# Opening of a fused adaLN kernel re-ordered: x loaded in place, one-time steps moved, gates and weight rounding in 35 steps

## The reference, cut to what matters

```python
# x: (8, 1024, 128); DEPTH = 6 layers; HEADS = 8
mod = (silu(c) @ wmod).reshape(8, 6, 1, -1)      # sa, ca, ga, sb, cb, gb
ga = (2 * (ga >= 0) - 1) * maximum(abs(ga), 0.25)   # "gates"; the same for gb
h = layernorm(x) * (1 + ca) + sa                 # "front norm", once per batch
for i in range(6):                               # linear attention + MLP
    xn = layernorm(h, ln1_w[i], ln1_b[i])
    q, k, v = xn @ wq[i], xn @ wk[i], xn @ wv[i]
    h = linear_attn(softmax(q), softmax over rows(k), v) @ wo[i] + bo[i] + h
    hdn = leaky_relu(layernorm(h, ln2_w[i], ln2_b[i]) @ w1[i])
    h = hdn @ w2[i] + h
x = x + ga * h
h = layernorm(x) * (1 + cb) + sb
x = x + gb * fp4_ffn(h)      # activations and w_gate, w_up, w_down rounded to FP4 in blocks of 16
```

## Time and profile before

| engine | busy us | share of the span |
|---|---|---|
| PE, matmul | 1163.3 | 88% |
| DVE | 1137.0 | 86% |
| POOL | 1128.7 | 85% |
| ACT | 957.0 | 72% |

### The profile page before, as it was taken

The page is one execution under the profiler, slowest core; times in us unless marked ns, Lnnn a source line. Parts: engine busy times, 40 slices in busy tenths (PEclk is TensorE's granted clock), DMA queues, the critical chain, the costliest instruction groups (busy, mean ns, idle before and its releaser), DMA issues.

```text
span 1327.5 us, 29895 instructions
## 1 busy us (share of the span) xinstructions
PE 1163.3 (88%) x9878; PEld 897.3 (68%) x9878; DVE 1137.0 (86%) x2872; ACT 957.0 (72%) x1578; POOL 1128.7 (85%) x1133
## 2 busy tenths in 40 slices
PE   6246889889999999999999999999999827888996
PEld 5233677667877887788778778877887613555564
DVE  5799899999998999999999999999986237998983
ACT  4345867778888888888888888888888725666753
POOL 3568897879998999999999999999977679999963
PEclk8568899999999999999999999999999967999998
DMA  6255444546555654556555555555553001010000
GB/s 218 85 159 143 129 127 142 149 143 181 160 176 175 184 176 154 165 168 191 152 168 160 178 166 174 160 172 158 176 169 108 2 32 32 17 48 17 18 32 32
DMA packets 117528, 172.38 MB, mean 130 GB/s; under 512 B 12577, under 2 KB 94849, under 8 KB 117377
## 3 DMA queue, kind: packets, MB, share of 16 engines
q1 hardware_dynamic: 117376, 170.48, 42.1%
HBM read 90.73 MB, written 79.69 MB: 128 GB/s over the span
## 4 chain that ended last, share of the span: by engine, by line
PE 66%; POOL 14%; issue 11%; DVE 5%; ACT 4%; DMA 0%; POOLq 0%; DVEq 0%; ACTq 0%
PE pair L485 5%; PE pair L514 5%; PE ring_pair L536 5%; PE ring_pair L538 5%; PE ring_pair L537 5%; PE pair_mlp L494 5%; PE pair_mlp L473 5%; PE pair_mlp L551 3%; PE pair_mlp L552 3%; PE pair_mlp L553 3%; PE ring_pair L524 3%; PE mlp L551 3%; PE mlp L552 3%; PE mlp L553 3%; POOL arena L1474 3%
## 5 line engine op out<-in xcount | busy, mean ns | idle before, releaser
L1494 POOL TENSOR_TENSOR hidden<-hidden 128x2048 f16<-128x2048 f32 x96 | 393.6, 4100 | 51.4 <-ACT hidden L743 51.2
L736 ACT ACTIVATE hidden<-ring_pair,hidden_bias 128x512 f32<-128x512 f32 x384 | 253.1, 683 | 55.1 <-PE ring_pair L538 43.3
L743 ACT ACTIVATE hidden<-hidden 128x2048 f16<-128x2048 f32 x96 | 182.9, 1905 | 2.3 <-PE mlp L553 0.7
L1432 POOL TENSOR_TENSOR rstd<-ve,minus_half 128x8 f32<-128x8 f32 x104 | 173.5, 1668 | 9.9 <-DVE ve L932 6.4
L912 DVE BATCH_NORM_STATS2 bn<-x_all 128x6 f32<-128x128 f32 x832 | 169.7, 275 | 5.1
L1474 POOL TENSOR_SCALAR arena<-x_all,rstd,nmr 128x128 f32<-128x128 f32 x384 | 165.7, 448 | 5.7 <-POOL nmr L1466 0.8
L536 PE MATMUL ring_pair<-arena,halves 128*128 128x512 f16 x384 | 146.8, 382 | 12.8 <-ACT hidden L736 12.3
L716 ACT ACTIVATE arena<-x_all,nmr,rstd 128x128 f32<-128x128 f32 x384 | 152.5, 483 | 0.0
L538 PE MATMUL ring_pair<-arena,halves 128*128 128x512 f16 x384 | 146.8, 382 | 0.0
L537 PE MATMUL ring_pair<-arena,halves 128*128 128x512 f16 x384 | 146.8, 382 | 0.0
L551 PE MATMUL mlp<-halves,hidden 128*128 128x128 f16 x768 | 137.4, 222 | 9.5 <-issue 9.5
(11 more groups left out here) (200 smaller groups left out, 3197.0 us busy)
## 6 DMA issues: line engine op xcount, KB each, us to landing
n_away<-n_blocks SPq DMA_DIRECT2D x48, 512.0 KB, 2.9
norm_raw<-n_away SPq DMA_DIRECT2D x192, 128.0 KB, 3.5
k_away<-k_blocks SPq DMA_DIRECT2D x48, 512.0 KB, 4.1
arena<-k_away SPq DMA_DIRECT2D x192, 128.0 KB, 3.5
q_away<-q_blocks SPq DMA_DIRECT2D x48, 512.0 KB, 2.9
arena<-q_away SPq DMA_DIRECT2D x192, 128.0 KB, 3.4
x_in<-in_L_attn_x SPq DMA_DIRECT2D x16, 512.0 KB, 3.8
out_x<-x_all SPq DMA_DIRECT2D x8, 512.0 KB, 2.6
```

Of the source, the lines that this page charges most:

```text
L736: act.activation(hidden_t[:, c * W + h * HALF:c * W + (h + 1) * HALF], ring[n % 2], ACT.Prelu, bias=hidden_bias[:, b:b + 1], scale=HIDDEN_ ...
L743: act.activation(half_rows(hidden_hi, h), half_rows(hidden_t, h), ACT.Copy).then_inc(hidden_hi_ready, 1)
L1432: return pool.tensor_tensor(rstd[:, 0:tiles], ve[:, 0:tiles], minus_half[:, 0:tiles], ALU.pow).then_inc(rstd_ready, 1)
L1494: pool.tensor_tensor(half_rows(hidden_lo, h), half_rows(hidden_t, h), half_rows(hidden_hi, h), ALU.subtract).then_inc(hidden_lo_ready, 1)
```

## The change

- x goes straight to its place in `x_all`; all eight loads are issued at the start. The front norm works in place. `front_stats` takes `bn_aggr` in place of six small operations; POOL computes variance + epsilon and the negated mean.
- SP: the loads of w1, wv, wo and layer 0 now stand ahead of w2; layer 1's weights too are loaded at the start. The feed-forward weights are loaded in turn 9. Batches 0 and 1 are loaded again in turns 32 and 33, one each.
- The one-time steps of all engines stand at other places of turns 0 to 4; the low parts of the MLP weights come in four groups of three.
- The rounding of the feed-forward weights is cut in 17 steps (halves of 128x560), one in each DVE turn 10 to 26; the gates in 18 steps (halves of 128x512), one in each turn 28 to 45. Each step stands between `shift_q` and `mask_context`.
- POOL's first feed-forward phase waits for 18 gate steps (9 before).

The diff, cut to its core:

```diff
-            for b in range(2):
-                sp.dma_start(x_in[:, b * W:(b + 1) * W], x_rows[b]).then_inc(x_loaded[b], 16)
+            def load_rows(b):
+                sp.dma_start(x_all[:, b * W:(b + 1) * W], x_rows[b]).then_inc(x_loaded[b] if b < 4 else x_rest_loaded, 16)
...
+            for b in range(2):
+                load_rows(b)
+            load_first()
+            load_values()
             load_layer(0)
+            for b in range(2, 4):
+                load_rows(b)
+            for l in range(DEPTH):
+                load_second(l)
+            load_bias()
+            for b in range(4, B):
+                load_rows(b)
+            load_layer(1)
+
+            def load_back(b):
+                if b == 0:
+                    sp.wait_ge(f_w_steps, W_STEPS)
                 else:
-                    sp.wait_ge(x_rest_loaded, 16 * (b - 2))
-                    sp.wait_ge(front_hat_ready, b - 2)
-                load_x(b).then_inc(x_rest_loaded, 16)
+                    sp.wait_ge(x_back_loaded, 16 * b)
+                load_x(b).then_inc(x_back_loaded, 16)
...
-                if v == 1:
-                    load_layer(1)
-                if v % B == 3 and 1 <= v // B < DEPTH - 1:
-                    load_layer(v // B + 1)
-                if v == 2 * B:
-                    sp.wait_ge(front_ready, B)
-                    sp.wait_ge(f_w_steps, W_STEPS)
-                    load_x(0).then_inc(x_back_loaded, 16)
-                    sp.wait_ge(x_back_loaded, 16)
-                    load_x(1).then_inc(x_back_loaded, 16)
+                if v == 9: load_gated()
+                if v % B == 3 and 1 <= v // B < DEPTH - 1: load_layer(v // B + 1)
+                if 32 <= v < 34: load_back(v - 32)
...
# DVE, front_stats
-                bn_rows(lambda t: x_in[:, bass.ds((b % 2) * W + t * D, D)], bn0, T, bn0_done)
-                sums(bn0, T, bn0_done, mean0_steps, b)
-                means(mean0, T, mean0_steps, b, sign=-1)
-                variances(ve0, T, mean0_steps, ve0_ready, b)
+                bn_rows(lambda t: x_all[:, bass.ds(b * W + t * D, D)], bn0, T, bn0_done)
+                moments(bn0, mv0, bn0_done, mv0_ready, b)
...
# DVE, a rounding step: halves of the columns, one operation a step
+            def round_weights(step):
...
+                elif step < 7:
+                    nc.vector.tensor_tensor(blocks(w), blocks(w), spread(inv, n_w // 2), ALU.mult).then_inc(f_w_steps, 1)
...
# DVE, items(v)
+                if v == 0: front_stats(1)
                 if on(v - 3): inverse_q(v - 3)
-                if 4 <= v < 8: prepare_gates((v - 4) // 2, v % 2 * 2)
...
+                if v == 2: prepare_downs()
+                if v == 3: front_stats(6)
                 if on(v - 3): block_q(v - 3)
                 if on(v): bn1_rows(v)
-                if v == 1: front_stats(3)
-                if 2 <= v < B - 2: front_stats(v + 2)
+                if v == 2: prepare_scales()
                 if on(v): moments1(v)
-                if v == 0: front_stats(1)
                 if v == 0: front_stats(2)
                 if v == 0: weight_bounds(1)
+                if v == 1: weight_bounds(0)
+                if v == 1: front_stats(3)
+                if v == 1: output_bias()
+                if v == 1: prepare_bounds()
...
                 if on(v - 2): max_q(v - 2)
+                if v == 2: prepare_weights(0, range(0, 3))
                 if on(v - 3): affine_z(v - 3)
                 if on(v - 2): shift_q(v - 2)
+                if v == 2: front_stats(5)
+                if v == 4: prepare_weights(1, range(0, 3))
+                if 10 <= v < 10 + W_STEPS: round_weights(v - 10)
+                if 28 <= v < 28 + GATE_STEPS: prepare_gates(v - 28)
                 if on(v - 3): mask_context(v - 3)
+                if v == 3: prepare_weights(0, range(3, DEPTH))
+                if v == 3: front_stats(7)
                 if on(v - 4): second_norm_low(v - 4)
+                if v == 4: prepare_weights(1, range(3, DEPTH))
...
-                if v == 1: prepare_weights(0, range(DEPTH))
-                if v == 2: prepare_weights(1, range(DEPTH))
-                if 4 <= v < 8: prepare_gates((v - 4) // 2, v % 2 * 2 + 1)
-                if v == 8: weight_scales()
-                if v == 9: weight_exponents()
-                if v == 10: weight_rounding()
# POOL, items(v)
+                if v == 0: front_root(1)
...
-                if v == 0: front_root(1)
+                if v == 0: front_rows(1)
                 if v == 0: front_root(2)
-                if v == 0: front_rows(1)
-                if 1 <= v < B - 1: front_rows(v + 1)
-                if 1 <= v < B - 2: front_root(v + 2)
+                if v == 1: front_root(3)
+                if v == 1: front_rows(2)
...
```

More of the change, by code:

```diff
@@ L750, in front_hat @@
                         act.wait_ge(rstd0_ready, b + 1)
-                    last = act.activation(x_all[:, bass.ds(b * W + t * D, D)], x_in[:, bass.ds((b % 2) * W + t * D, D)], ACT.Identity,
+                    last = act.activation(x_all[:, bass.ds(b * W + t * D, D)], x_all[:, bass.ds(b * W + t * D, D)], ACT.Identity,
                                           scale=rstd0[:, t:t + 1], bias=nmr0[:, t:t + 1])
@@ L767, in prepare_weights @@
                     act.wait_ge(w1_folded, 1)
-                for l in range(DEPTH):
+                else:
+                    act.wait_ge(w2_loaded, 16 * DEPTH)
+                for l in layers:
                     c = n * DEPTH + l
@@ L869, in items @@
                 if on(v - 1): exp_k(v - 1)
+                if v == 1: prepare_weights(0, range(0, 3))
+                if v == 1: front_hat(4)
+                if v == 2: front_hat(5)
+                if v == 2: prepare_weights(0, range(3, DEPTH))
+                if v == 3: prepare_weights(1, range(3, DEPTH))
                 if on(v - 4): copy_hidden(v - 4, 6)
@@ L875, in items @@
                 if on(v - 1): exp_q(v - 1)
+                if v == 2: prepare_weights(1, range(0, 3))
+                if v == 3: front_hat(7)
                 if on(v - 4): hidden_high(v - 4, 1)
@@ L913, in bn_rows, with moments @@
                 last.then_inc(bn_done, 1)
-            def sums(bn, tiles, bn_done, steps, n):
-                part = bn[:, 0:6 * tiles].rearrange("p (t k) -> p k t", k=6)
-                total, gap, square = (a[:, 0:tiles] for a in (row_total, row_gap, row_square))
+            def moments(bn, mv, bn_done, mv_ready, n):
                 dve.wait_ge(bn_done, n + 1)
-                nc.vector.tensor_tensor(total, part[:, 1], part[:, 4], ALU.add).then_inc(steps, 1)
-                nc.vector.tensor_tensor(gap, part[:, 1], part[:, 4], ALU.subtract).then_inc(steps, 1)
-                nc.vector.scalar_tensor_tensor(out=square, in0=part[:, 2], scalar=D * LN_EPS, in1=part[:, 5],
-                                               op0=ALU.add, op1=ALU.add).then_inc(steps, 1)
@@ L924, in means @@
-            def means(mean, tiles, steps, n, sign=1):
-                total, gap = row_total[:, 0:tiles], row_gap[:, 0:tiles]
-                dve.wait_ge(steps, 5 * n + 3)
-                nc.vector.tensor_scalar(mean[:, 0:tiles], total, 0.5 * sign, None, ALU.mult).then_inc(steps, 1)
-                nc.vector.scalar_tensor_tensor(out=gap, in0=gap, scalar=0.25, in1=gap, op0=ALU.mult, op1=ALU.mult).then_inc(steps, 1)
-            def variances(ve, tiles, steps, ve_ready, n):
-                dve.wait_ge(steps, 5 * n + 5)
-                nc.vector.scalar_tensor_tensor(out=ve[:, 0:tiles], in0=row_square[:, 0:tiles], scalar=1.0 / D,
-                                               in1=row_gap[:, 0:tiles], op0=ALU.mult, op1=ALU.add).then_inc(ve_ready, 1)
+                for t in range(T):
+                    last = nc.vector.bn_aggr(mv[:, 2 * t:2 * t + 2], bn[:, 6 * t:6 * t + 6])
@@ L961, in front_apply @@
                 last.then_inc(front_ready, 1)
-            def moments(bn, mv, bn_done, mv_ready, n):
-                dve.wait_ge(bn_done, n + 1)
-                for t in range(T):
-                    last = nc.vector.bn_aggr(mv[:, 2 * t:2 * t + 2], bn[:, 6 * t:6 * t + 6])
-                last.then_inc(mv_ready, 1)
             def bn1_rows(i):
@@ L1102, in prepare_gates @@
                 if step == 0:
                     dve.wait_ge(mod_out_copied, B)
-                    after(dve, mod_out_steps, 5 * n)
+                else:
+                    dve.wait_ge(mod_out_steps, step)
+                if k == 0:
                     nc.vector.tensor_scalar(size, g, -1.0, GATE_FLOOR, ALU.mult, ALU.max).then_inc(mod_out_steps, 1)
-                    if n == 0:
-                        nc.vector.tensor_scalar(cb, cb, 1.0, None, ALU.add).then_inc(mod_out_steps, 1)
-                elif step == 1:
-                    dve.wait_ge(mod_out_steps, 4 * n + 2)
+                elif k == 1:
```

176 lines of the change are left out of this document (96 added, 80 removed).

## The result

The changed kernel takes 1279.74 us (median of 4 runs, 1277.25 to 1282.66) against 1329.97 (4 runs, 1329.17 to 1332.89): a ratio of 0.9619, 95% interval 0.9594 to 0.9644. The profiled execution took 1282.66 us, span 1280.9, and is the slowest of the four.

A forecast was written before the change was run, and what follows sets the result against it. PE was taken to bound the steady items (19.09 us each), with DVE near full in the first seven. 16 + 26.6 + 2.2 - 3 = 41.8 off the 1327.5 us span gave 1285.7, forecast 1288 us, range 1277 to 1314.

The forecast's parts named there:

- Term A: Opening: the first MLP product starts at 103 instead of 119.40 us; gain 16 us (bounds 8 to 18).
- The walk: Hand trace of the opening's new lists with old durations: first MLP product at 101.2, plus 2, taken as 103.
- Term B: Items 0 to 7: without gates and rounding 139.5 us against 166.1; gain 26.6 (bounds 15 to 32.4).
- PE becomes the bound: Early items without gates and rounding: DVE's 17.6 and 17.1 us lie below PE's 20.6 and 20.9, so PE limits.
- Term C: SP's second load of x no longer waits: the item of 21.31 us falls to 19.09, 2.2 us gained.
- Term D: The 35 short steps in steady items: each waits for one POOL tile (0.43 us); cost 3 us in all.
- Rival (2): Steady items: POOL's eight tiles hold each step to their end, `context_out` 2.0 us late: 1345 us; chance 0.12.
- Rival (3): Steady items: each step costs its length, 21 us more, 1306 us; chance 0.20 together with another rival.

The follow-up runs named there:

- e1: The kernel before, with the short steps and the back loads of x in turns 32 and 33, its opening untouched: 1305.41 us, ratio 0.9812.
- e2: The changed kernel with the gates and weight rounding in long whole steps in turns 4 to 10, as in the kernel before: 1303.43 us, ratio 0.9797.
- e6: The changed kernel's storage, loads, front norm and short steps, with the opening's one-time steps in the order of the kernel before: 1305.33 us, ratio 0.981.
- e3: The changed kernel with both back loads of x in turn 32: 1282.82 us, ratio 0.964.
- e4: The changed kernel with each short step at the end of its DVE turn, beside a long POOL operation: 1330.13 us, ratio 0.9995.
- e7: The changed kernel with one more DVE operation in each of turns 10 to 45, beside the short steps: 1284.26 us, ratio 0.9652.
- e9: The changed kernel with the front steps of images (batches) 6 and 7 alone at their old, later turns: 1285.72 us, ratio 0.9654.
- e11: The changed kernel with the one-time steps on the weights alone in the order of the kernel before: 1283.97 us, ratio 0.9643.
- e8: The changed kernel with image 7's statistics, root and product one turn later and w2's six low parts behind `second_norm_low`: 1288.69 us, ratio 0.9678.
- e13: The changed kernel with w2's six low parts behind `second_norm_low` and image 7's front steps alone late on all engines: 1282.49 us, ratio 0.964.

## Why the prediction was right, point by point

**Term A, right in size.** Expected 16, measured 119.40 - 103.41 = 16.0. The walk had `block_n` at 28.5, 43.0, 62.3 and 82.3; the trace has 28.91, 43.30, 65.38 and 84.39, so the 2 us added for meetings with POOL were needed. Three low parts took 3.21 at 98.72, and in turn 2 an operation of 6 columns stood to the end of a pass of `front_rows` (one of 12 columns had taken 1.31 beside the pass before):

```profile
53.71 2.36 POOL L1464 TENSOR_TENSOR x_all<-x_all,mod_in 128x1024 f32<-128x1024 f32 x1
53.91 2.19 DVE L1167 SCALAR_TENSOR_TENSOR mlp_up<-ups 128x6 f32<-128x6 f32 x1
```

That the agreement is to a tenth is luck: equal openings start item 0 anywhere from 100.72 to 102.24, and the 2 us were a guess at the number of meetings. The order is not all of the term: the gates moved alone bring item 0 0.8 earlier (e1), and moved back 2.0 later (e2). That the swap of storage saves nothing is shown by e6 against e1 for the old order only.

**Term B, right in size, its cause only in part.** Expected 26.6 for the seven items, measured 166.12 - 137.66 = 28.5. I put it to the gates and the rounding. e1 and e2 give these 19.5 and 19.8. e6 gives the order 9.7 in the same items (with some overlap in the sum). The step of the text that missed this is "PE becomes the bound": without the gates, but with the old order, POOL is (23.94 of 24.42 in e1), since the front work of the last images lies in turns 5 and 6. I read the low clock of the earlier trace rows as given; with POOL's work out of the way PE is full and its clock 1.00 from item 1, where I had taken 20.5 for items 1 and 2. In the sum this is partly hidden: items 1 and 2 came out 2.8 us shorter than taken, but item 0 1.1 longer (22.59 for 21.5).

**Term C, right.** 2.2 expected and seen (21.31 to 19.09); undone in e3, one item is 21.40 again and the stretch of items 14 to 44 2.1 us longer.

**Term D, too large.** Expected 3 us, seen 0: 572.83 in both kernels. I took a wait of one POOL tile a step. The trace shows the reverse: DVE starts its step without a wait, and POOL's tile is stretched (0.43 to 1.03), which POOL has time for (540.15 of 572.83). Rival (2) fails at this place for that reason, but its mechanism is real one POOL operation later: e4 pays 50 us. Rival (3) falls with e7.

**The sum.** The forecast of 1288 was 8.3 us too high; apart from the tail's 0.3, every term that missed did so toward a larger gain than forecast. Term B gave 1.9 more, the items between 7 and 14 0.2, term D 3.0, the tail took 0.3: 4.8 of span, 1280.9 for 1285.7. Of the other 3.5 us, 2.9 is that the profiled run lay above its median.

**Open.** Of the order's 25.6 us, e9 and e11 undo 10 when taken singly (6.5 of 24.8 by the start of item 3). The rest belongs to images 2 to 5 or to both parts together; that was not separated.

## What to carry to other kernels

Work that must be done once is free in a steady stage if each piece is no longer than the idle time that one turn has on its engine, and if it stands beside short operations of GpSimd and not beside a long one: the same 35 steps cost 0 or 50 us by their place alone. When a long piece is taken out of a stretch, look which engine is full next, since a late front step on GpSimd reached TensorE through ScalarE's queue. A saving at the first item is real only if the work taken from ahead of it does not land in the items behind it (e8, e9, e13).
